# One product instead of two in the feed-forward of a batch-by-batch kernel, and the next batch's heads made earlier in the round

## The chip, the cores and the metric

The kernel runs on one core of one Trainium2 chip. The metric is the device time in microseconds of one execution. The kernel before was run three times. One further execution was profiled, and every row below comes from it.

## The reference, cut to what matters

An input x of 8 batches, 512 tokens and 256 features goes through four layers, each with a residual sum: an RNN, an LSTM, an attention block with a feed-forward, and a block of experts. The change is in the third. There a vector is mapped by `logmap0` and `expmap0`, which scale it by a function of its norm; between two such steps only a factor for each token is left.

```python
def plin(x, w, b):
    return expmap0(logmap0(x) @ w + b)
...
q = _to_heads(plin(xm, w_q, b_q))          # k and v alike
...
attn_out = plin(_from_heads(out_h), w_o, b_o)
x = mobius_add(residual, expmap0(g_msa * logmap0(attn_out)))
residual = x
xn = layer_norm(logmap0(x))
xm = expmap0(xn * (1 + sc_mlp) + sh_mlp)
ff = plin(plin(xm, w_f1, b_f1), w_f2, b_f2)   # w_f1 [256, 1024], w_f2 [1024, 256]
return mobius_add(residual, expmap0(g_mlp * logmap0(ff)))
```

There is no non-linear function between the two feed-forward matrices. With z = logmap0(xm) and u = z W1 + b1, the second `plin` needs u W2, a row of 256 for each token, and the norm of u, one number for each token. The last layer passes all tokens through a shared expert and through two of four further experts, chosen for each batch; each has a 256x1024 and a 1024x256 matrix.

## The kernel before, in words

The first part of the program (to about 1200 us) runs both recurrences and makes the attention's inputs. The second part works in nine rounds. Round b makes the attention block of batch b (called front, rounds 0 to 7) and the experts of batch b-1 (rounds 1 to 8) together. Nothing is scheduled by a planner: each engine has one function (`tensor_round`, `vector_round`, `scalar_round`, `gpsimd_round`, `sync_round`), and the order of its lines is the order of the engine's queue. Engines meet at named semaphores: `pe.wait_ge(*at("zsT_hi", b))` waits until the instruction that raises `zsT_hi` in round b is done.

A batch's 512 tokens are NQ = 4 tiles (q) of 128 partitions. The 256 features are KC = 2 blocks (k), the 1024 hidden units FC = 8 blocks (m). `steps`, `up` and `down` are the experts' products, 24 of each in a round; TensorE takes them between the front's own steps. A round goes as follows:

- Attention: scores (L1368), exponentials (L2032), values (L1383), transposes of the results, up to `o_t`, with which z is complete.
- Transposes, the product by wo (L1435), then a long chain on VectorE (`mobius_products`, `mobius_factors`, `mobius_sum`, then the norm: `moments`, `log_norm`, `normalise`, `norm_ratio`). ScalarE helps with squares, tanh and logarithm, GpSimd with powers (L2111). The result is z, scaled for each token (L1889).
- Transposes of z (L1314), copied to zT by ScalarE (first half, L2053) and VectorE (second half, L1891).
- Feed-forward: for each m two products of 512 columns, W1 against zT (L1478), ScalarE's bias (L2057) and square (L2059), VectorE's running sum of the squares (L1901), and four products of 256 columns with W2 (L1470). At the end four products with a column of ones add the squares over the partitions (L1489).
- Beside the feed-forward the next batch's heads are made: squares (L1971), sums (L1727, L1735), the power, roots (L1975), factors (L1740 to L1758), values (L2143), scaled q and k (L1764), their high parts in fp16 (L1982) and low parts (L1772).
- A second mobius chain gives the block's output (L1929, `x_out`). TensorE transposes the high and low parts (L1353, `split_transposes`), and the copies of these (`splT_moved`) are what the next round's scores wait for.

The heads' squares are written over the tiles of the attention's results (`hsq`, `oT` and `O` share `spl`), so they can't be made before z is complete. Round 0 has no experts' products; there `kept_busy` puts products that nobody reads into the longest waits. 

## Time and profile before

| | us |
|---|---|
| median of three runs | 2486.86 (2485.87 to 2488.44) |
| profiled execution, first to last instruction | 2483.3 |
| median less that span | 3.6 |
| TensorE busy in the profile | 2358.1 (95%) |
| VectorE busy | 1570.9 (63%) |
| ScalarE busy | 1350.9 (54%) |
| GpSimd busy | 569.8 (23%) |
| mean granted clock of TensorE | 0.991 |
| HBM traffic | 39 GB/s over the span |

The profiled execution's own time is known only as its span; what lies around it is not listed apart. Busy times overlap between engines. Matmuls are pipelined, so their durations overlap too, and starts are the better measure.
### The profile page before, as it was taken

To read this page: it belongs to the slowest core of one execution; us is meant where nothing else is said; L and a number is where in the kernel's file an instruction comes from. 1 tells how busy PE (TensorE), PEld (TensorE's weight loads), DVE (VectorE), ACT (ScalarE), POOL (GpSimd) and SP (SyncE) were. 2 spreads that over 40 slices of the span, in tenths; PEclk is the share of its full clock that TensorE was granted. 3 is DMA by queue.
4 is the path that set the end of the run, shared out by engine and by line. 5 is a ranking of instruction groups with operands and counts; after the bars stand their busy time and mean duration, and the time that the engine had idled before them with its cause. 6 is when DMAs were issued, how large, how long until landed. Compare 5 with 4: busy or idle time off the path is not lost.

```text
span 2483.3 us, 96145 instructions
## 1 busy us (share of the span) xinstructions
PE 2358.1 (95%) x39648; PEld 1570.9 (63%) x39648; DVE 1570.9 (63%) x7207; ACT 1350.9 (54%) x4515; POOL 569.8 (23%) x1177
## 2 busy tenths in 40 slices
PE   8899999999999999999868999999999999999999
PEld 6677777777777777776333665646556465564666
DVE  5777777777777877777466546546465464655330
ACT  4555555555555555555748556565555665556432
POOL 0222222332223222232222203222031221212100
PEclk9999999999999999999979999999999999999999
DMA  4111111110000000000103002030020301102020
GB/s 114 33 36 42 32 40 42 32 30 25 30 27 29 27 27 30 26 23 15 65 0 115 1 14 110 0 124 1 33 92 1 124 1 52 72 1 98 1 81 9
DMA packets 51880, 102.74 MB, mean 41 GB/s; under 512 B 10468, under 2 KB 33380, under 8 KB 47348
## 3 DMA queue, kind: packets, MB, share of 16 engines
q1 hardware_dynamic: 48036, 94.06, 11.2%
q8 instruction: 315, 5.16, 0.9%
q10 hardware_dynamic: 3408, 2.52, 0.3%
q14 instruction: 121, 0.99, 0.1%
HBM read 75.53 MB, written 21.04 MB: 39 GB/s over the span
## 4 chain that ended last, share of the span: by engine, by line
PE 42%; DVE 4%; ACT 3%; issue 2%; POOL 1%; DVEq 0%; ACTq 0%
PE bank L1262 13%; PE bank L1276 12%; PE bank L1470 4%; PE bank L1478 4%; ACT pexp L2032 2%; PE bank L1383 2%; PE bank L1368 1%; PE bank L1435 1%; PE bank L1297 1%; POOL hs L2111 1%; PE bank L1353 1%; PE bank L1314 1%; DVE x L1595 0%; DVE x L1598 0%; DVE spl L1786 0%
## 5 line engine op out<-in xcount | busy, mean ns | idle before, releaser
L135 PE MATMUL psFI<-wh,Hs 128*8 128x128 f32 (+3 forms) x8192 | 324.8, 276 | 60.5 <-DVE Hs L250 47.1
L135 PE MATMUL psOR<-wh,RH 128*16 128x128 f32 (+3 forms) x8320 | 321.4, 272 | 2.5 <-ACT RH L338 2.1
L135 PEld LDWEIGHTS psFI<-wh,Hs 128*8 128x8 f32 (+3 forms) x8192 | 182.2, 99 | 178.9 <-DVE Hs L250 178.4
L2032 ACT ACTIVATE pexp<-bank 128x1024 f32<-128x1024 f32 x256 | 244.2, 1022 | 33.8 <-PE bank L1368 33.6
L338 ACT ACTIVATE RH<-RT 128x16 f32<-128x16 f32 x512 | 111.0, 217 | 261.3 <-DVE RT L254 261.3
L1262 PE MATMUL bank<-x3T,ew 128*128 128x512 f32 x512 | 239.2, 594 | 0.0
L329 ACT ACTIVATE sFI<-FIT 128x32 f32<-128x32 f32 x512 | 118.6, 232 | 200.3 <-DVE FIT L234 195.5
L234 DVE STREAM_TRANSPOSE FIT<-psFI 128x128 f32<-128x128 f32 x512 | 162.3, 317 | 101.0 <-PE psFI L135 98.5
L135 PEld LDWEIGHTS psOR<-wh,RH 128*16 128x16 f32 (+1 forms) x8320 | 205.6, 104 | 5.1 <-ACT RH L338 3.7
L135 PE MATMUL psG<-wh,Hs 128*8 128x64 f32 (+3 forms) x8192 | 208.3, 219 | 0.0
L1276 PE MATMUL bank<-ew,hidden 128*128 128x256 f32 x864 | 201.0, 379 | 0.0
L1276 PEld LDWEIGHTS bank<-ew,hidden 128*128 128x128 f32 x864 | 163.5, 190 | 53.5 <-issue 35.4
L2111 POOL TENSOR_TENSOR hs<-hs,half 128x16 f32<-128x16 f32 x32 | 92.9, 2904 | 371.8 <-DVE hs L1799 371.8
L782 PE MATMUL psB<-wqkv,zrT 128*128 128x128 f32 x720 | 175.8, 326 | 0.0
L135 PEld LDWEIGHTS psG<-wh,Hs 128*8 128x8 f32 (+3 forms) x8192 | 174.7, 100 | 0.0
L135 PE MATMUL psOR<-wx,XX 128*32 128x128 f32 (+1 forms) x4160 | 168.8, 278 | 2.4 <-DMA XX<-in_xT 2.4
L335 ACT ACTIVATE tC<-cc 128x16 f32<-128x16 f32 x512 | 111.3, 217 | 104.7 <-DVE cc L243 103.7
L1951 ACT ACTIVATE hidden<-bank,eb1s 128x512 f32<-128x512 f32 x128 | 87.5, 684 | 130.9 <-PE bank L1262 129.1
L2111 POOL TENSOR_TENSOR S<-acc,half 128x4 f32<-128x4 f32 (+2 forms) x47 | 69.4, 1477 | 376.0 <-ACT dump L1964 138.1
L782 PEld LDWEIGHTS psB<-wqkv,zrT 128*128 128x128 f32 x720 | 107.0, 188 | 72.9 <-issue 70.4
L1262 PEld LDWEIGHTS bank<-x3T,ew 128*128 128x128 f32 x512 | 95.8, 190 | 73.7 <-issue 68.9
L250 DVE TENSOR_TENSOR Hs<-oT,tC 128x16 f32<-128x16 f32 x512 | 90.4, 177 | 75.7 <-ACT tC L335 1.5
(358 smaller groups left out, 4631.3 us busy)
## 6 DMA issues: line engine op xcount, KB each, us to landing
ew<-in_ew SPq DMA_DIRECT2D x32, 1024.0 KB, 9.6
qkv_scratch<-qkvr SPq DMA_DIRECT2D x31, 384.0 KB, 2.7
big<-qkv_scratch SPq DMA_DIRECT2D x7, 1536.0 KB, 7.6
XX<-in_xT SPq DMA_DIRECT2D x31, 256.0 KB, 2.7
x_scratch<-xr SPq DMA_DIRECT2D x32, 128.5 KB, 2.4
x<-x_scratch SPq DMA_DIRECT2D x8, 514.0 KB, 8.8
ada<-ada_scratch SPq DMA_DIRECT2D x8, 512.0 KB, 8.4
out_x<-x SPq DMA_DIRECT2D x7, 512.0 KB, 3.3
```

The costliest lines, as they stand in the source:

```text
L135: last = pe.matmul(bank[32 * j:32 * j + width, :], state(k), weights[:, k, j, cols], start=False, stop=k == KC - 1, tile_position=(0, 32 * ...
L234: dve.transpose(flat(R.FIT), R.psFI[g % 2]).then_inc(sem["fiT"], 1)
L329: act.activation(R.sFI[:, :, :, 1].rearrange("p g (k b) -> p (g k) b", k=KC), R.FIT[:, :, at_four:at_four + NB], ACT.Sigmoid).then_inc(sem ...
L335: act.activation(R.tC[:, :, :], by_block(second_scan(R.cc)), ACT.Tanh).then_inc(sem["tC"], 1)
L338: act.activation(r_of(i), R.RT[:, :, at_pair:at_pair + NB], ACT.Tanh).then_inc(sem["tR"], 1)
L782: last = pe.matmul(self.psB[:, half * P:(half + 1) * P], self.zT[:, k, :], self.wqkv[:, k, n * D + half * P:n * D + (half + 1) * P], start ...
L1262: last = pe.matmul(bank(4 + i % 2), M.expert(n)[0][:, k, m * P:(m + 1) * P], M.x3T[:, k, :], start=k == 0, stop=k == KC - 1)
L1276: last = pe.matmul(y_bank(q), M.hidden[:, i % HIDDEN, q * P:(q + 1) * P], M.expert(n)[1][:, m, :], start=m == 0 and (y_bank == M.last_bank ...
L1470: last = pe.matmul(bank(2 + q // 2)[:, (q % 2) * D:(q % 2 + 1) * D], M.uT[:, m, q * P:(q + 1) * P], W["wf2"][:, m, :], start=(m == 0 and q ...
L1478: last = pe.matmul(bank(m % 2), W["wf1"][:, k, m * P:(m + 1) * P], M.zT[:, k, :], start=k == 0, stop=k == KC - 1)
L2032: up(act.activation(M.pexp[:, n % 2, 2 * pr:2 * pr + 2, :], M.PS[pr][:, :, :], ACT.Exp, scale=1.0 / math.sqrt(HD)), "exps")
L2111: pool.tensor_tensor(out, base, exponent, ALU.pow).then_inc(M.sem(name), 1)
```

## The change

The feed-forward keeps one matrix of 1024 rows and 512 columns, `wf` = [W2 | W1 transposed], in place of the two. In round 0 TensorE multiplies it by W1 once: `gram` = W1 [W2 | W1 transposed], 256 x 512, kept in SBUF for all batches. The bias gives two rows, b1 W2 and 2 b1 W1-transposed, and one number, b1 b1. Each batch then takes four times two products of zT with `gram`. The left 256 columns are z W1 W2, to which a row is added. The right 256, multiplied by z and added up, are the square of the norm of z W1, to which VectorE adds the bias's part.

The heads' work is moved on VectorE, ScalarE and GpSimd: squares and sums beside the product by wo, roots and factors into the norm, the values and the scaled q and k before the copy of zT, high parts behind it, low parts between the second `mobius_factors` and `mobius_sum`. The squares' unread results now go over the exponentials' tile. Round 0's copies of the transposes are split as in the other rounds (five of eight on VectorE).

```diff
+    def gram(k):
+
+        for m in range(FC):
+            last = pe.matmul(bank(4 + k), W["wf"][:, m, D + k * P:D + (k + 1) * P], W["wf"][:, m, :], start=m == 0, stop=m == FC - 1)
+        last.then_inc(M.sem("gram_ps"), 1)
+
+    def gram_of_bias():
+
+        pe.wait_ge(*at("wide", b))
+        for m in range(FC):
+            last = pe.matmul(bank(6), M.bias_wide[:, m, :], W["wf"][:, m, :], start=m == 0, stop=m == FC - 1)
+        last.then_inc(M.sem("gram_ps"), 1)
+        for m in range(FC):
+            last = pe.matmul(bank(7)[:, 0:1], M.bias_wide[:, m, :], W["bf1"][:, m:m + 1], start=m == 0, stop=m == FC - 1)
+        last.then_inc(M.sem("gram_ps"), 1)
...
-            if a == 0 and hp2 in (0, 2):
-                pe.wait_ge(*at("a" if hp2 else "ss_f", batch - 1))
+            if a == 0:
+                pe.wait_ge(*at("ff_bias", batch - 1, hp2 + 1))
...
         output_transposes(0)
         back(H // 4 - 1)
+        if not experts:
+            gram(0)
...
         if not experts:
-            pe.wait_ge(*at("ratio2", b))
-            kept_busy(2)
+            gram(1)
+            gram_of_bias()
+            pe.wait_ge(*at("gram", b))
...
-        def second(m):
-            pe.wait_ge(*at("u", b, m + 1))
-            for q in range(NQ):
-                last = pe.matmul(bank(2 + q // 2)[:, (q % 2) * D:(q % 2 + 1) * D], M.uT[:, m, q * P:(q + 1) * P], W["wf2"][:, m, :],
-                                 start=(m == 0 and q % 2 == 0), stop=m == FC - 1, skip_group_check=True)
-            return last
-
-        for m in range(FC):
-            if m >= 2:
-                pe.wait_ge(*at("u", b, m - 1))
+        for q in range(NQ):
             for k in range(KC):
-                last = pe.matmul(bank(m % 2), W["wf1"][:, k, m * P:(m + 1) * P], M.zT[:, k, :], start=k == 0, stop=k == KC - 1)
-            last.then_inc(M.sem("u_ps"), 1)
-            if m:
-                second(m - 1)
+                last = pe.matmul(bank(q), M.zT[:, k, q * P:(q + 1) * P], M.gram[:, k, :], start=k == 0, stop=k == KC - 1)
+            last.then_inc(M.sem("ff_ps"), 1)
         if experts:
             up(FC + LEAD + 3)
-        second(FC - 1).then_inc(M.sem("ff_ps"), 1)
-        if experts:
             down(FC + 3)
-        pe.wait_ge(*at("u_ss", b))
-        for q in range(NQ):
-            last = pe.matmul(bank(0)[:, q:q + 1], M.uss[:, q * P:(q + 1) * P], M.ones[:, 0:1], start=q == 0, stop=True, skip_group_check=True)
-        last.then_inc(M.sem("utot_ps"), 1)
         if experts:
...
+        heads = b + 1 < NB
+        if heads:
+            for q in range(NQ):
+                head_sums(b + 1, q)
+            head_totals(b + 1)
...
         normalise(N, z, M.ada25[:, 1, :], b)
+        if heads:
+            head_factors(b + 1)
         norm_ratio(N, b)
         dve.wait_ge(C.sem, C.n)
         for q in range(NQ):
             up(dve.tensor_scalar(z[:, q, :], z[:, q, :], N.s1[:, q:q + 1], None, ALU.mult), "zs")
+        if not experts:
+            dve.wait_ge(*at("gram", b))
+        for q in range(NQ):
+            dve.wait_ge(*at("zs", b, q + 1))
+            if q:
+                dve.wait_ge(C.sem, C.n)
+            C.link(dve.tensor_tensor_reduce(out=M.dump_dve[:, :], in0=z[:, q, :], in1=M.ff_rows[:, D:], scale=1.0, scalar=M.bias_square[:, :],
+                                            op0=ALU.mult, op1=ALU.add, accum_out=S[:, 9, q:q + 1]))
+        if heads:
+            for q in range(NQ):
+                scaled(b + 1, q)
         dve.wait_ge(*at("zsT_ps", b, 2))
         up(dve.tensor_copy(M.zT[:, 1, :], bank(1)), "zsT_hi")
...
+        def linear_outputs(q):
+
+            dve.wait_ge(*at("ff_ps", b, q + 1))
+            dve.wait_ge(C.sem, C.n)
+            C.link(dve.tensor_tensor_reduce(out=M.dump_dve[:, :], in0=z[:, q, :], in1=bank(q)[:, D:], scale=1.0, scalar=S[:, 9, q:q + 1],
+                                            op0=ALU.mult, op1=ALU.add, accum_out=acc[:, 7, q:q + 1]))
+            up(dve.tensor_tensor(M.w[:, q, :], bank(q)[:, 0:D], M.ff_rows[:, 0:D], ALU.add), "ff_bias")
+
+        for q in range(NQ):
+            linear_outputs(q)
+        dve.wait_ge(C.sem, C.n)
+        up(dve.tensor_scalar(acc[:, 7, :], acc[:, 7, :], 0.0, None, ALU.max), "ss_f")
...
         mobius_factors(M.norm2.X2, 1)
+        if heads:
+            for q in range(NQ):
+                low_parts(b + 1, q)
         mobius_sum(1)
         for q in range(NQ):
             if q == 0:
                 dve.wait_ge(C.sem, C.n)
             up(dve.tensor_tensor(M.x1[:, q, :], M.x1[:, q, :], M.x[b % 2][:, q, :], ALU.add), "x_out")
-        if heads and experts:
+        if heads:
             for a, hp2 in SPLIT_B:
                 splT_moved(b + 1, a, hp2)
...
+        hidden(1, 2, 3)
+        if b + 1 < NB:
+            act.wait_ge(*at("o_t", b))
+            for q in range(NQ):
+                heads_squared(b + 1, q)
+        hidden(4)
+        if not experts:
+            gram_moved(0)
         mobius_squares(0, lambda: None)
         hidden(5, 6)
         tanh(0)
+        if not experts:
+            gram_moved(1)
         mobius_scaled(M.x[b % 2], 0)
         hidden(7, 8)
         logarithm(M.norm2, b)
+        if b + 1 < NB:
+            head_roots(b + 1)
+            act.activation(M.exp_scratch[:, :], M.mhalf[:, 0:1], ACT.Gelu_apprx_tanh)
+        if not experts:
+            bias_rows_moved()
...
-        for m in range(FC):
-            act.wait_ge(*at("u_ps", b, m + 1))
-            up(act.activation(M.uT[:, m, :], bank(m % 2), ACT.Identity, bias=W["bf1"][:, m:m + 1]), "u")
-            act.wait_ge(*at("u", b, m + 1))
-            up(act.activation(M.usq[:, m, :], M.uT[:, m, :], ACT.Square), "u_sq")
-            if b + 1 < NB:
-                if m < 2:
-                    heads_squared(b + 1, 2 * m)
-                    heads_squared(b + 1, 2 * m + 1)
-                if m == 2:
-                    head_roots(b + 1)
-                    act.activation(M.exp_scratch[:, :], M.mhalf[:, 0:1], ACT.Gelu_apprx_tanh)
-                if m >= 5:
-                    high_parts(b + 1, m - 5)
         if b + 1 < NB:
-            high_parts(b + 1, NQ - 1)
+            for q in range(NQ):
+                high_parts(b + 1, q)
...
+    if front and not experts:
+        pool.tensor_copy(M.bias_wide, M.W["bf1"][:, :].unsqueeze(2).to_broadcast([P, FC, P])).then_inc(M.sem("wide"), 1)
     if front:
         for g in range(H // 4):
             power(M.hs[:, 2, :, 4 * g:4 * g + 4], M.hs[:, 0, :, 4 * g:4 * g + 4], M.half[:, 0:4 * NQ].rearrange("p (q h) -> p q h", h=4), at("ss_o", b, g + 1), "root_o")
         power(S[:, 8, :], acc[:, 7, :], root, at("ss_t", b), "pow_o")
+        if b + 1 < NB:
+            head_norms(b + 1)
...
```

VectorE takes out of its queue the seven sums of squares (L1901) and the interleaving of the heads' steps with them.

TensorE's queue around the feed-forward of round 1, before. `z` and `zT` are the block's rows and their transposes, `ew_0` an expert's weights, `pexp` holds the hidden units u.

```order
L1314 MATMUL bank<-I,z 128x128
L1276 MATMUL bank<-ew_0,hidden 128x256 [waits s_hidden]
L1276 MATMUL bank<-ew_0,hidden 128x256 x3
L1478 MATMUL bank<-zT,W_wf 128x512 [waits s_zsT_hi,s_zsT_lo]
L1478 MATMUL bank<-zT,W_wf 128x512 x3
L1470 MATMUL bank<-W_wf,pexp 128x256 [waits s_u]
L1470 MATMUL bank<-W_wf,pexp 128x256 x3
L1478 MATMUL bank<-zT,W_wf 128x512 [waits s_u]
L1478 MATMUL bank<-zT,W_wf 128x512
```

The same place now:

```order
L1314 MATMUL bank<-I,z 128x128
L1276 MATMUL bank<-ew_0,hidden 128x256 [waits s_hidden]
L1276 MATMUL bank<-ew_0,hidden 128x256 x3
L1488 MATMUL bank<-gram,zT 128x512 [waits s_zsT_hi,s_zsT_lo]
L1488 MATMUL bank<-gram,zT 128x512 x7
L1262 MATMUL bank<-x3T,ew_0 128x512 [waits s_hidden]
L1262 MATMUL bank<-x3T,ew_0 128x512
```

Sixteen and thirty-two products have become eight, with the same wait ahead of them, and the experts follow at once.

VectorE's queue from the norm to the copy of zT in a round with experts, before. `S` and `hs` hold factors for each token and head, `big` is the next batch's q, k and v.

```order
L1659 SCALAR_TENSOR_TENSOR z<-z,S,ada 128x256 x4
L1663 TENSOR_SCALAR S<-S 128x4
L1516 RECIPROCAL S<-S 128x4
L1518 SCALAR_TENSOR_TENSOR S<-S 128x4
L1889 TENSOR_SCALAR z<-z,S 128x256 x4
L1891 COPY zT<-bank 128x512
```

The same stretch now, the first and last of the nine factor instructions and one of the four sums shown:

```order
L1661 SCALAR_TENSOR_TENSOR z<-z,S,ada 128x256 x4
L1742 TENSOR_SCALAR S<-S 128x4x3
...
L1760 TENSOR_TENSOR hs<-hs,S 128x192
L1665 TENSOR_SCALAR S<-S 128x4
L1518 RECIPROCAL S<-S 128x4
L1520 SCALAR_TENSOR_TENSOR S<-S 128x4
L1898 TENSOR_SCALAR z<-z,S 128x256 x4
L1905 ISA dump_dve,S<-z,ff_rows,bias_square 128x256
L1905 ISA S 128x1
...
L1766 TENSOR_TENSOR big<-big,hs 128x256 x8
L1911 COPY zT<-bank 128x512
```

The factors stand ahead of the ratio, and the sums against the bias row and all eight scalings ahead of the copy.

TensorE in round 0 from z's last transposes to the feed-forward, before and now:

```order
L1326 MATMUL bank<-I,z 128x128 x4
L1435 MATMUL bank<-W_wo,zT 128x256 x8
L1321 MATMUL bank<-W_wf 128x512 x5
L1314 MATMUL bank<-I,z 128x128 x8
```

```order
L1326 MATMUL bank<-W_wf 128x512 x8
L1342 MATMUL bank<-I,z 128x128 x4
L1453 MATMUL bank<-W_wo,zT 128x256 x8
L1326 MATMUL bank<-W_wf 128x512 x8
L1333 MATMUL bank<-W_wf,hidden 128x512 x8
L1336 MATMUL bank<-W_bf,hidden 128x1 x8
L1321 MATMUL bank<-W_wf 128x512 x3
L1314 MATMUL bank<-I,z 128x128 x8
```

The products of the matrices stand ahead of z's last transposes and behind the product by wo, in place of two of the five unread ones.

## Rows read from the trace of the kernel before

**Rows 1.** Stretches of round 2: length, each engine's busy time, granted clock, DMA share, GB/s.
```profile
1472.00:1513.00 41.00, 38.32 (x261) 13.23 (x260) 22.53 (x76) 34.18 (x39) 6.86 (x3) 1.00 0.52 187
1513.00:1626.00 113.00, 113.00 (x462) 76.61 (x461) 63.24 (x193) 57.56 (x121) 25.48 (x22) 1.00 0.00 1
```

**Rows 2.** Timeline of TensorE, round 2: start us, us, engine, line, what, count.
```profile
1559.21 3.60 PE L1478 MATMUL bank<-zT,W_wf 128*128 128x512 f32 x8
1562.64 1.89 PE L1470 MATMUL bank<-W_wf,pexp 128*128 128x256 f32 x8
1564.37 1.88 PE L1478 MATMUL bank<-zT,W_wf 128*128 128x512 f32 x4
...
1585.03 1.88 PE L1262 MATMUL bank<-x3T,ew 128*128 128x512 f32 x4
1586.74 1.89 PE L1470 MATMUL bank<-W_wf,pexp 128*128 128x256 f32 x8
1588.47 1.89 PE L1276 MATMUL bank<-ew,hidden 128*128 128x256 f32 x8
1590.20 0.95 PE L1489 MATMUL bank<-ones_,uss 128*128 128x1 f32 x8
1591.01 1.96 PE L1262 MATMUL bank<-x3T,ew 128*128 128x512 f32 x4
...
1611.75 1.95 PE L1353 MATMUL bank<-I,spl 128*128 128x128 f16 x32
```

**Rows 3.** Timeline of VectorE, round 2, with the idle time before.
```profile
1525.82 1.66 DVE L1668 SCALAR_TENSOR_TENSOR z<-bank,S,W_bo 128x256 f32<-128x256 f32 x4 [3.98 <-PE bank L1435]
...
1549.87 0.69 DVE L1663 TENSOR_SCALAR S<-S 128x4 f32<-128x4 f32 x1 [2.82 <-POOL S L2111]
...
1551.27 2.05 DVE L1889 TENSOR_SCALAR z<-z,S 128x256 f32<-128x256 f32 x4
1557.68 0.69 DVE L1891 COPY zT<-bank 128x512 f32<-128x512 f32 x1 [4.36 <-PE bank L1314]
...
1565.94 1.81 DVE L1727 TENSOR_REDUCE hs<-spl 128x48 f32<-128x768 f32 x2
...
1577.20 1.61 DVE L1764 TENSOR_TENSOR big<-big,hs 128x256 f32<-128x256 f32 x2
...
1580.85 1.28 DVE L1772 TENSOR_TENSOR spl<-big,spl 128x512 f16<-128x512 f32 x2
...
1582.65 0.75 DVE L1764 TENSOR_TENSOR big<-big,hs 128x256 f32<-128x256 f32 x2
```

**Rows 4.** Stretches of round 2 cut at VectorE's instructions, columns as in rows 1.
```profile
1528.73:1531.03 2.30, 2.30 (x11) 1.80 (x10) 1.73 (x9) 1.48 (x7) 1.31 (x1) 1.00 0.00 0
1572.95:1576.68 3.73, 3.73 (x15) 2.52 (x14) 3.45 (x11) 1.38 (x3) 0.00 (x0) 1.00 0.00 0
1591.18:1606.88 15.70, 15.70 (x53) 9.98 (x53) 12.07 (x49) 9.18 (x30) 3.91 (x4) 1.00 0.00 0
```

**Rows 5.** Timeline of ScalarE, round 2.
```profile
1542.36 0.21 ACT L2004 ACTIVATE S<-S 128x4 f32<-128x4 f32 x1 [0.78 <-DVE S L1637]
...
1562.38 1.56 ACT L1971 ACTIVATE spl<-big 128x768 f32<-128x768 f32 x2
```

**Rows 6.** Timeline of GpSimd, round 2.
```profile
1549.81 2.84 POOL L2120 TENSOR_TENSOR x<-x,weighted 128x256 f32<-128x256 f32 x4
...
1576.76 3.55 POOL L2143 TENSOR_TENSOR vt<-big,hs 128x256 f32<-128x256 f32 x4 [5.80 <-DVE hs L1758]
```

**Rows 7.** Timeline of TensorE, round 0.
```profile
1245.84 1.11 PE L1326 MATMUL bank<-I,z 128*128 128x128 f32 x4 [6.26 <-DVE z L1816]
```

**Rows 8.** Stretches of round 0, columns as in rows 1.
```profile
1248.00:1250.00 2.00, 2.00 (x5) 1.64 (x6) 0.16 (x1) 0.00 (x0) 0.00 (x0) 0.50 0.00 0
1277.50:1306.95 29.45, 28.57 (x104) 19.21 (x104) 20.51 (x37) 21.18 (x33) 6.21 (x5) 1.00 0.00 1
1306.95:1321.90 14.95, 9.60 (x70) 5.92 (x70) 12.78 (x51) 12.76 (x30) 3.02 (x2) 0.67 0.42 142
```

More of the change, by code:

```diff
@@ L420, in __init__ @@
         self.of = {}
-        for name, shape in (("wo", [P, KC, D]), ("wf1", [P, KC, FF]), ("wf2", [P, FC, D]),
+        for name, shape in (("wo", [P, KC, D]), ("wf", [P, FC, 2 * D]),
                             ("sw1", [P, KC, FF]), ("sw2", [P, FC, D]), ("gate_w", [P, 3 * KC, E]),
@@ L1320, in kept_busy @@
         for _ in range(n):
-            pe.matmul(bank(4), W["wf1"][:, 0, 0:P], W["wf1"][:, 1, 0:T], start=True, stop=True)
+            pe.matmul(bank(4), W["wf"][:, 0, 0:P], W["wf"][:, 1, :], start=True, stop=True)
+    def gram(k):
[10 more added lines that the diff above has]
+        last.then_inc(M.sem("gram_ps"), 1)
     def output_transposes(k):
@@ L1664, in norm_ratio, with mobius_products @@
         C.link(clipped_ratio(N.s1, N.n_, N.t0, C))
-    def mobius_products(banks, bias, gate, xa, nth):
+    def mobius_products(made, bias, gate, xa, nth):
         for q in range(NQ):
-            up(dve.scalar_tensor_tensor(z[:, q, :], bank(banks[q // 2])[:, (q % 2) * D:(q % 2 + 1) * D], S[:, 7, q:q + 1], bias[:, :], ALU.mult, ALU.add), "a")
+            up(dve.scalar_tensor_tensor(z[:, q, :], made(q), S[:, 7, q:q + 1], bias[:, :], ALU.mult, ALU.add), "a")
         for q in range(NQ):
@@ L1892, in vector_round @@
     if front:
-        heads = b + 1 < NB
-        if heads:
-            head_sums(b + 1, 0)
-            head_sums(b + 1, 1)
-        for m in range(1, FC):
-            dve.wait_ge(*at("u_sq", b, m + 1))
-            if m > 1:
-                dve.wait_ge(*at("u_ss", b, m - 1))
-            up(dve.tensor_tensor(M.uss, M.usq[:, 0, :] if m == 1 else M.uss, M.usq[:, m, :], ALU.add), "u_ss")
-            if heads and m == 1:
-                head_sums(b + 1, 2)
-                head_sums(b + 1, 3)
-                head_totals(b + 1)
-            if heads and m == 3:
-                head_factors(b + 1)
-            if heads and m >= 4:
-                scaled(b + 1, m - 4)
-            if heads and m >= 5:
-                low_parts(b + 1, m - 5)
-        if heads and experts:
-            low_parts(b + 1, NQ - 1)
-        dve.wait_ge(*at("utot_ps", b))
-        up(dve.tensor_copy(acc[:, 7, :], bank(0)[:, 0:NQ]), "ss_f")
-        if heads and not experts:
-            low_parts(b + 1, NQ - 1)
+        def linear_outputs(q):
[8 more added lines that the diff above has]
+        up(dve.tensor_scalar(acc[:, 7, :], acc[:, 7, :], 0.0, None, ALU.max), "ss_f")
         dve.wait_ge(*at("pow_f", b))
@@ L1929, in vector_round @@
             up(dve.tensor_tensor(M.x1[:, q, :], M.x1[:, q, :], M.x[b % 2][:, q, :], ALU.add), "x_out")
-        if heads and experts:
+        if heads:
             for a, hp2 in SPLIT_B:
@@ L2013, in splT_moved, with gram_moved, bias_rows_moved @@
         for a, hp2 in groups:
-            if batch == 1 or (a, hp2) not in SPLIT_B:
+            if (a, hp2) not in SPLIT_B:
                 act.wait_ge(*M.of_heads("splT_ps", batch, 4 * a + hp2 + 1))
                 up(act.copy(M.splT[:, a, 2 * hp2:2 * hp2 + 2, :].rearrange("p j t -> p (j t)"), bank(hp2).bitcast(fp16)), "splT_B" if (a, hp2) in SPLIT_B else "splT_A")
+    def gram_moved(k):
+        act.wait_ge(*at("gram_ps", b, k + 1))
+        up(act.copy(M.gram[:, k, :], bank(4 + k)), "gram")
+    def bias_rows_moved():
+        act.wait_ge(*at("gram_ps", b, 4))
+        up(act.copy(M.ff_rows[:, 0:D], bank(6)[:, 0:D]), "gram")
+        up(act.activation(M.ff_rows[:, D:], bank(6)[:, D:], ACT.Identity, scale=2.0), "gram")
+        up(act.copy(M.bias_square[:, :], bank(7)[:, 0:1]), "gram")
     def x3T_moved():
@@ L2087, in scalar_round @@
         hidden(19, 20)
-        if experts and b + 1 < NB:
+        if b + 1 < NB:
             splT_moved(b + 1, (0, 0), (0, 2))
         hidden(21, 22)
-        if experts and b + 1 < NB:
+        if b + 1 < NB:
             splT_moved(b + 1, (1, 0))
@@ L2148, in gpsimd_round @@
         power(S[:, 8, :], acc[:, 7, :], root, at("ss_t", b), "pow_o")
+        if b + 1 < NB:
+            head_norms(b + 1)
         mobius_power(0)
```

36 lines of the change are left out of this document (14 added, 22 removed).

## Prediction

> **What bounds the kernel now.** I read the stretches of one steady round first, then TensorE's timeline in it, then VectorE's, ScalarE's and GpSimd's, then round 0. A round lies between the first score product of one batch and that of the next. Its first 41 us (attention) are shared: TensorE is busy for 38.32 us and ScalarE for 34.18. In the next 113 us TensorE is busy for 113.00 us, VectorE for 63.24, ScalarE for 57.56, at a granted clock of 1.00 (the 2.4 GHz level) and with no transfers [rows 1]. So in the part of the round that the change touches TensorE alone sets the time, and what leaves its queue is worth its full length, as long as the others still hand over in time. Seven of the nine rounds (1 to 7) have this shape; round 0 has no experts' products to lie beside the chain, and round 8 has no feed-forward.
>
> **What leaves TensorE in a steady round.** I go by start to start, since the durations overlap. The feed-forward's first products start at 1559.21 and the experts' next one at 1585.03: 25.82 us. Its last second-stage group takes from 1586.74 to 1588.47, 1.73 us, and the sums of squares from 1590.20 to 1591.01, 0.81 us. Together 28.36 us [rows 2]. (Each fp32 matmul stands twice in the trace: x8 are four of them.) In their place come eight fp32 products 512 wide with a 128x128 stationary tile. Four such take from 1559.21 to 1562.64, 3.43 us [rows 2], so eight take 6.86. TensorE's queue gets 28.36 - 6.86 = 21.50 us shorter. As TensorE is without a gap there, that is the gain, less what it now waits.
>
> **What is late next: the second half of zT.** TensorE needs VectorE's copy of zT before the new product. Before, it arrived at 1559.21 and did not wait [rows 2]. VectorE now has more ahead of that copy. Term by term, in round 2:
> - Squares of the next heads' input: 1.56 us for two on ScalarE [rows 5], 3.1 for four, in the gap before the product by wo is done. VectorE idles there for 3.98 us [rows 3] and now reduces four times 0.905 (1.81 for two [rows 3]), and one small total. It ends about 0.3 us after 1525.82. Bounds: 0 if it fits, 1.5 if each sum waits for its square. I take 0.3.
> - Factors: the nine instructions take 3.73 us [rows 4]. They go before the ratio, where VectorE idles for 2.82 us on GpSimd's power [rows 3]. The part that doesn't fit is 0.9, and with the first 0.3 and GpSimd's additions beside it I take 1.5 for the two items together. ScalarE's root, with two table loads, goes after its logarithm at 1542.36 [rows 5]; it pushes two Gelus by some 2 us and the four squares of the norm by about 0.3, which is less than VectorE's own delay. TensorE needs these Gelus two steps later, so I cost them at nothing; uncovered, they would be 1.9.
> - Four products with a sum, against the bias row: 2.30 us for four of this kind [rows 4].
> - Eight scalings: 0.75 for two with GpSimd quiet, so 3.0; 1.61 for two beside its values' products, so 6.4 [rows 3, 6].
> - Then the copy, 0.69 [rows 3], as it was.
> The scaling of z starts at 1551.27 and takes 2.05 us with GpSimd busy [rows 3, 6]. So: 1551.27 + 1.5 + 2.05 + 2.30 + 3.0 + 0.7 + some 0.2 of handing over = 1561.0, which is 1.8 us after 1559.21. GpSimd's products for the values (3.55 us [rows 6]) now start once its additions end, near 1553, and lie on the end of the scaling of z and on the sums instead of on the eight scalings. I add 0.7 for it: TensorE waits 2.5 us in each of rounds 1 to 6. Bounds: 1.0 (no disturbance, squares fit) and 6.0 (all eight scalings at the disturbed price).
>
> On that disturbance: two scalings took 0.75 us alone and 1.61 beside GpSimd [rows 3, 6]. The Trainium skill (SBUF — State Buffer, Who interferes with whom) says that a VectorE instruction with two SBUF inputs and a GpSimd instruction that reads SBUF exclude each other for the whole instruction. The trace agrees with it in direction. By that rule alone the sums against the bias row would each be blocked too, and the wait would come out near 3.5 us and not 2.5, worth 6 us over six rounds; it is inside the range.
>
> **Is the rest in time?** The four outputs q are consumed while the next product runs: about 1.1 us of VectorE each (0.57 for the sum [rows 4], an addition at the price of a scaling, 0.38 [rows 3], and handing over) against 1.7 us of TensorE. The sum of squares is then ready at 1559.2 + 2.5 + 6.9 + 1.2 = 1569.8 instead of 1591.18, 21.4 us earlier. From it to the block's output VectorE takes 15.70 us [rows 4], and the low parts now lie inside it: eight at 0.64 (1.28 for two [rows 3]), 5.1 us. The low parts end about 1587. TensorE reaches their transposes at 1611.75 - 19.0 = 1592.7 [rows 2]: 6 us of slack, so I cost this move at nothing; if the low parts came 10 us later it would be 4 us a round. ScalarE loses sixteen instructions and gets the casts back, from 57.56 busy in 113 [rows 1]. Weights and the next batch's input arrive within the attention part, DMA share 0.52 there and 0.00 after it [rows 1], so the earlier squares find their input.
>
> So a round with next heads gains 21.50 - 2.5 = 19.0 us, six times: 114.0. Round 7 makes no heads: only the sums are added, 2.3 us on VectorE against the 4.36 us that it idled for the transposes [rows 3]. It gains 21.5.
>
> **Round 0.** Here the chain through VectorE sets the end, and nothing lies beside it.
> - Eight of the products of the matrices start where TensorE idled for 6.26 us [rows 7] and take 6.86: 0.6 late. But TensorE then enters the product by wo without having idled. Before, it was granted 0.50 (1.2 GHz) there [rows 8], after that idle time. The transposes and this product gain some 1.5. VectorE's four sums limit it, so I take 0.5 gained in all.
> - The others (eight, and eight with the bias, 13.7 us, and eight small ones) lie beside the norm, where only products that are thrown away stood. ScalarE's three small copies of them come ahead of its squares of the norm; at no more than the 0.69 us of the copy of zT each they are 2.1 us, and the factors' 1.5 us on VectorE cover most of it. Nothing, at the most 0.6.
> - From the copy of zT to the sum of squares: 29.45 us before [rows 8]. The copy comes later by 1.5 (factors) + 0.9 (scaling of z, now beside GpSimd, an estimate: half of its 2.05) + 2.3 + 3.0 = 7.7, less the 0.5: 7.2. TensorE idles for it, and part of the new product may run at 1.2 GHz: 6.86 + 2. With the last outputs, 1.2, and the copy with its handing over, 0.9, it is 7.2 + 8.9 + 1.2 + 0.9 = 18.2. Gain 11.2.
> - From the sum of squares to the next scores: 14.95 us before [rows 8]. The low parts (5.1) and VectorE's five copies of the transposes, done early before, now come into it; a copy at the 0.69 of zT's [rows 3] makes 3.4. Loss 8.5.
> Round 0: about 2.7 gained; between 8 lost (the product wholly at 1.2 GHz, the copies one behind the other) and 7 gained.
>
> **Sum.** 114.0 + 21.5 + 2.7 = 138.2 us. The profiled execution's span is 2483.3 us, giving 2345.1; the median of the runs is 3.6 above that span, which I take as fixed: 2486.9 - 138.2 = 2348.7 us.
>
> **Rivals.**
> - The clock falls in the new wait. In the steady rounds TensorE never waits as long as in my forecast, and after 6.26 us without work its clock was 0.50 [rows 7, 8]. Were it to fall at each wait for zT, the new product would take 13.7 us and not 6.9: 6 x 6.9 = 41 us lost, 2390 us. Against it: the gap is under half of that one. The Trainium skill (TensorE: Matmul & The Clock Gate, HAM oscillation — how this bites in real kernels) says that a wait in every iteration can make every next burst start cold. Whether 2.5 us do it no row here shows.
> - VectorE takes over the end of the round: the low parts or the output come after TensorE has reached their transposes. For it: all the heads' work that lay beside 28 us of products is now beside the norm and 7 us. Against it: the 6 us of slack. With 10 us more on VectorE, 4 us are lost in six rounds: 2373 us.
> - Slower than before: the clock falls at that wait and stays at 1.2 GHz. The 138 us gained are used up once 138 / 6 = 23 us of work in each of six rounds run at half speed. Behind the wait stand 1626.0 - 19.0 - (1559.2 + 2.5) = 45 us of the round [rows 1, 2]; were all of it at that level, the loss would be 6 x 45 = 270 us: about 2619. Against it: TensorE has work without a gap after the wait, and in round 0 the clock was back at 1.00 over the stretch from the copy of zT on [rows 8].
> - The shorter queue is not what the time follows, because something else had to arrive anyway: about 2480 us. The 113.00 of 113.00 speaks against it [rows 1].
>
> **Chances.** Forecast 0.81, clock at each wait 0.07, VectorE at the end 0.08, slower 0.02, nothing gained 0.02. The forecast's own range comes from its bounds: waits of 1.0 to 6.0 us (9 less, 21 more) and round 0 (4 less, 11 more): 2335 to 2380. I hold 2334 to 2378, which leaves out the first rival and a bit of the forecast. This kernel's measurement can't tell less than 0.2% (5 us) from no change. Faster 0.97, the same 0.01, slower 0.02.
>
> **What would show it.** In the changed profile: L1488's eight products in about 6.9 us, then the experts at once; an idle time of TensorE of about 2.5 us before them in rounds 1 to 6, ended by VectorE's copy of zT, and none in round 7; a clock of 1.00 there; rounds of about 135 us where they were 41 + 113 [rows 1]; no wait before the split transposes of rounds 1 to 6; round 0 about as long as before. Wrong it would be if the wait for zT is over 6 us, if TensorE shows 0.50 in a steady round, or if it idles before the transposes of the low parts or of the block's output.

## The result and the profile after

The median went from 2487.0 to 2344.5 us (after: four runs, 2343.05 to 2345.88; before: four, 2485.87 to 2488.44), a ratio of 0.9425 (95% interval 0.9414 to 0.9436). That is 142.5 us less, where 138.2 were forecast; 2348.7 was predicted. The profiled execution's span is 2341.3 us, 142.0 less than before, at a mean granted clock of 0.991. TensorE is busy for 2207.2 us of it (94%), VectorE for 1581.1 (68%).

Where it went, by start times on TensorE: up to round 0's first score product 1.4 us were lost (1202.94 before, 1204.37 after; the other profiles scatter about as much). From there to round 1's product by wo 4.55 were gained. From that to round 7's product by wo it was 117.34, which is 19.56 for each of six rounds, and in the rest 21.54.

First the stretches of round 2 of the kernel after, in the columns of [rows 1]; the round now lasts from 1450.13 to 1584.19 us.

```profile
1450.00:1491.00 41.00, 38.68 (x259) 13.15 (x258) 23.20 (x77) 33.68 (x37) 7.87 (x3) 1.00 0.52 187
1491.00:1584.00 93.00, 91.20 (x375) 60.44 (x373) 63.79 (x206) 46.40 (x105) 23.42 (x22) 1.00 0.00 1
```

The attention part is as it was. The rest is 93 us instead of 113 [rows 1], TensorE is busy in 91.20 of them, and the missing 1.8 us are one wait. Here it is in TensorE's timeline, after, round 2 (start, duration, line, what, count, idle time before and who ended it):

```profile
1499.15 3.62 PE L1453 MATMUL bank<-W_wo,zT 128*128 128x256 f32 x16
...
1534.47 1.89 PE L1276 MATMUL bank<-ew,hidden 128*128 128x256 f32 x8
1538.16 7.11 PE L1488 MATMUL bank<-gram,zT 128*128 128x512 f32 x16 [1.80 <-DVE zT L1911]
1545.10 1.88 PE L1262 MATMUL bank<-x3T,ew 128*128 128x512 f32 x4
...
1569.20 1.95 PE L1369 MATMUL bank<-I,spl 128*128 128x128 f16 x32
```

The new product takes 6.94 us from start to start in place of the 28.36 of both old ones and the sums of squares [rows 2]. The transposes of the low parts (L1369) show no wait. The wait's 1.80 us are counted from the modelled end of the products before; start to start it costs 3.69 - 1.72 = 1.97, since eight such entries otherwise take 1.72. So 28.36 - 6.94 - 1.97 = 19.45, and the rounds show 19.56.

VectorE in the same round, after; what was beside 28 us of products now stands before the copy of zT:

```profile
1498.74 3.52 DVE L1729 TENSOR_REDUCE hs<-spl 128x48 f32<-128x768 f32 x4
1502.37 0.35 DVE L1737 TENSOR_REDUCE acc<-hs 128x12 f32<-128x192 f32 x1
1502.80 1.66 DVE L1670 SCALAR_TENSOR_TENSOR z<-bank,S,W_bo 128x256 f32<-128x256 f32 x4
...
1526.92 0.81 DVE L1758 SCALAR_TENSOR_TENSOR hs<-hs 128x192 f32<-128x192 f32 x1
1527.76 0.77 DVE L1760 TENSOR_TENSOR hs<-hs,S 128x192 f32<-128x192 f32 x1
1528.45 0.69 DVE L1665 TENSOR_SCALAR S<-S 128x4 f32<-128x4 f32 x1
...
1529.85 2.56 DVE L1898 TENSOR_SCALAR z<-z,S 128x256 f32<-128x256 f32 x4
1532.33 0.47 DVE L1905 CUSTOM_DVE_ANT_0 dump_dve<-z,ff_rows,bias_square 128x256 f32<-128x256 f32 x1
...
1534.64 2.77 DVE L1766 TENSOR_TENSOR big<-big,hs 128x256 f32<-128x256 f32 x8
1537.33 0.68 DVE L1911 COPY zT<-bank 128x512 f32<-128x512 f32 x1
...
1558.30 4.90 DVE L1774 TENSOR_TENSOR spl<-big,spl 128x512 f16<-128x512 f32 x8
```

GpSimd beside it, after:

```profile
1526.79 3.00 POOL L2135 TENSOR_TENSOR x<-x,weighted 128x256 f32<-128x256 f32 x4
1529.76 2.50 POOL L2160 TENSOR_TENSOR vt<-big,hs 128x256 f32<-128x256 f32 x4
```

The four sums of the squares end just before the first addition from the banks, which starts 3.65 us after the product by wo, as before (3.66). GpSimd's work now lies on the last factors and the scaling of z. The eight scalings of q and k run alone: 2.69 us from start to start, 0.34 each, where two took 1.61 beside GpSimd and 0.75 without [rows 3].

Round 0, TensorE after:

```profile
1240.88 7.03 PE L1326 MATMUL bank<-W_wf 128*128 128x512 f32 x16
1247.75 0.60 PE L1342 MATMUL bank<-I,z 128*128 128x128 f32 x4
1249.23 3.69 PE L1453 MATMUL bank<-W_wo,zT 128*128 128x256 f32 x16 [0.88 <-DVE zT L1870]
...
1273.35 5.49 PE L1321 MATMUL bank<-W_wf 128*128 128x512 f32 x6 [5.02 <-ACT bias_square L2038]
...
1286.33 8.77 PE L1488 MATMUL bank<-gram,zT 128*128 128x512 f32 x16 [5.26 <-DVE zT L1911]
1307.91 0.37 PE L1369 MATMUL bank<-I,spl 128*128 128x128 f16 x2 [12.80 <-DVE spl L1774]
```

The first matrix products fill the 6.26 us of [rows 7], and the product by wo takes 3.69 us. Before, it took 5.09, with a granted clock of 0.50 in its first 2 us [rows 8]. Against that stand two waits: 5.02 us for ScalarE's copies of the matrices, and 5.26 for zT, after which the new product takes 8.77 instead of 7.1. The stretch of the unread products behind the first of them shows the clock at 0.55, and ScalarE's timeline shows why the copies (L2036) are late: the early root stands in front of them, with a table load before it and one behind it:

```profile
1274.00:1280.00 6.00, 5.67 (x10) 1.85 (x8) 5.62 (x15) 0.89 (x6) 3.35 (x5) 0.55 0.00 0
```

```profile
1269.53 1.28 ACT L1986 ACT_TABLE_LOAD   x1
...
1271.21 1.28 ACT L2081 ACT_TABLE_LOAD   x1
1272.50 0.20 ACT L2081 ACTIVATE exp_scratch<-mhalf 128x1 f32<-128x1 f32 x1
1272.61 0.35 ACT L2036 COPY ff_rows<-bank 128x256 f32<-128x256 f32 x1
```

### The profile page after: what moved, and what is told of

Its sections match the earlier page's. It is cut to its first block and busy times, and to the rows that moved or that the text cites. A ratio compares the mean times of both kernels' runs of the same rounds, so it can differ in the third digit from the quotient of the medians.

```text
span 2341.3 us, 94850 instructions
## 1 busy us (share of the span) xinstructions
PE 2207.2 (94%) x39004; PEld 1452.3 (62%) x39004; DVE 1581.1 (68%) x7316; ACT 1257.8 (54%) x4381; POOL 560.5 (24%) x1178
## 5 line engine op out<-in xcount | busy, mean ns | idle before, releaser
L2054 ACT ACTIVATE pexp<-bank 128x1024 f32<-128x1024 f32 x256 | 244.3, 1023 | 36.1 <-PE bank L1384 35.9
L240 DVE TENSOR_TENSOR gw<-sFI,cc 128x16 f32<-128x16 f32 x512 | 90.4, 176 | 72.4 <-ACT sFI L329 3.0
```

The source lines that it names most:

```text
L240: dve.tensor_tensor(second_scan(R.gw), second_scan(R.sFI[:, 0]), second_scan(R.cc), ALU.mult).then_inc(sem["w"], 1)
L2054: up(act.activation(M.pexp[:, n % 2, 2 * pr:2 * pr + 2, :], M.PS[pr][:, :, :], ACT.Exp, scale=1.0 / math.sqrt(HD)), "exps")
```

## The experiments

All ten were run beside the kernel before (medians of 2486.2 to 2486.6 us in three sets of runs); ratios are to it. "After" is the changed kernel at 2344.5. "A round" is the distance between the products by wo of two rounds, 134.1 us in the kernel after.

### Does TensorE's queue set the rounds? (e1_product_twice)

```diff
         for q in range(NQ):
-            for k in range(KC):
-                last = pe.matmul(bank(q), M.zT[:, k, ...], M.gram[:, k, :], ...)
+            for _ in range(2):
+                for k in range(KC):
+                    last = pe.matmul(bank(q), M.zT[:, k, ...], M.gram[:, k, :], ...)
```

> The changed kernel, with each of the four pairs of products by gram taken twice (the second time to the same result). Theory, TensorE's queue sets the steady rounds: eight more products are 7.1 us in each of rounds 1 to 7 and some 7 to 9 in round 0, so 2344.5 + 57 = 2401 us, and rounds of 141.2 us where the changed kernel has 134.1. Rival, VectorE's chain behind the product is nearly as long as TensorE's queue: it is pushed by the same 7.1 us, so the time is the same, but TensorE then idles before the split transposes or the output's transposes. Rival, part of TensorE's time is hidden: less than 40 us in all, 2344 to 2384.

Measured: 2397.4 us (2396.26 to 2400.38), ratio 0.9644 (0.9628 to 0.966), 52.9 over after. TensorE, round 2:

```profile
1550.71 13.97 PE L1489 MATMUL bank<-gram,zT 128*128 128x512 f32 x32 [1.80 <-DVE zT L1912]
```

Five of the six rounds are 140.9 us, 6.8 longer. The sixth is 142.7; its doubled product ran slow (see the last section). The wait is the same, and none appears before the split transposes. By the profile the second part is 57.0 us longer, which is what was expected; the time shows 52.9, in part because what comes before the rounds was 1.8 us shorter in this execution. What is added to TensorE's queue is paid in full; so was what left it. The theory that something else had to arrive anyway is out.

### What the wait for zT costs (e2_scaled_after_copy, e3_both_after_copy)

e2 moves the eight scalings behind the copy of zT, e3 also the four sums against the bias row:

```diff
-        if heads:
-            for q in range(NQ):
-                scaled(b + 1, q)
         dve.wait_ge(*at("zsT_ps", b, 2))
         up(dve.tensor_copy(M.zT[:, 1, :], bank(1)), "zsT_hi")
+        if heads:
+            for q in range(NQ):
+                scaled(b + 1, q)
```

> The changed kernel, with VectorE's eight scalings of the next q and k behind its copy of zT instead of ahead of it. Theory, the 1.8 us that TensorE waits in rounds 1 to 6 and most of the 5.3 us of round 0 are these scalings standing ahead of the copy: the wait goes in rounds 1 to 6 (10.9 us), and in round 0 it falls by 2.5 to 3 and with it some of the product's slow clock: 2344.5 - 14 = 2330 us. Rival, the scalings then lie in front of VectorE's work on the outputs and cost there what they save here: 2340 to 2346. The four outputs take VectorE 4.4 us beside 7.1 us of products, so there is room for 2.7 us; I expect the first.

> As the run before, and the four sums against the bias row behind the copy too. Theory: in rounds 1 to 6 there is no wait left to take, so they stay; in round 0 the copy comes another 2.4 us earlier, and the product starts without its clock having fallen: 2330 - 2.4 - 1 = 2327 us. Rival, 5 us of VectorE behind the copy are more than the product hides, and the second chain starts later: then round 0 gains nothing over the run before (2330), while the steady rounds stay, having some 6 us of slack.

e2: 2328.6 us (2326.8 to 2329.1), 0.9365 (0.9349 to 0.9381), 15.9 less than after. Rounds 1 to 6 have no wait, and most are 132.0 to 132.1 us. TensorE, round 2 of e2:

```profile
1530.99 7.03 PE L1488 MATMUL bank<-gram,zT 128*128 128x512 f32 x16
```

A round is 2.05 us shorter: the wait's 1.97 and 0.08 of the product, which is 7.03 without a wait and 7.11 with one. Six times that is 12.3; round 0's wait fell from 5.26 to 2.57. e3: 2325.1 us (2322.93 to 2327.34), 0.9349 (0.9334 to 0.9365). Its times can't be told from e2's; in round 0 the wait is 0.88, but the product still takes 8.80. I had counted on it being faster there.

### Does the heads' early move pay, and how much slack was there? (e4, e8, e5, e6)

e4 keeps the new product but makes the heads late: sums behind the copy of zT, factors and scalings after the second norm's ratio, and on ScalarE squares, root and high parts in front of a Gelu, `hidden(14)`. e8 puts the high parts behind Gelus 14 to 16. The core of e4 against after, and of e8 against e4:

```diff
-        if heads:
-            head_factors(b + 1)
         norm_ratio(N, b)
...
+        if heads:
+            head_factors(b + 1)
+            for q in range(NQ):
+                scaled(b + 1, q)
         dve.wait_ge(*at("ff_bias", b))
...
         hidden(13)
         if b + 1 < NB:
             for q in range(NQ):
+                heads_squared(b + 1, q)
+            head_roots(b + 1)
+            act.activation(M.exp_scratch[:, :], M.mhalf[:, 0:1], ACT.Gelu_apprx_tanh)
+            for q in range(NQ):
                 high_parts(b + 1, q)
         hidden(14)
```

```diff
-            for q in range(NQ):
-                high_parts(b + 1, q)
         hidden(14)
         mobius_squares(1, lambda: hidden(15))
         hidden(16)
+        if b + 1 < NB:
+            for q in range(NQ):
+                high_parts(b + 1, q)
         tanh(1)
```

> The changed kernel's single product, but the next heads made behind the copy of zT, as before the change (squares and sums beside the product, factors and scalings ahead of the second chain). Theory, the single product gives the gain and the heads' move only a little: no wait for zT (1.8 us gained), but the low parts end about 4 us after TensorE reaches their transposes: 2 us lost a round, and some 2 in round 0: 2344.5 + 14 = 2358 us. Rival, the heads' work needs the product's old length as cover, so that without the move half of the gain is lost: 10 us a round, 2344.5 + 65 = 2410 us.

> As the run with the heads made late, but ScalarE's high parts behind the experts' Gelus 14 to 16 and not ahead of them. In that run TensorE waited 5.7 us a round for a Gelu (34.8 us), which stood behind the high parts, which waited for VectorE's scalings. Theory, that place in ScalarE's queue was the loss: without it only the 2 us a round that I had expected are left, from the low parts: 2355 to 2365 us. Rival, VectorE's heads' work behind the copy is what is too long: the wait turns up ahead of the split transposes instead, 5 us a round, and the time stays at 2377.

e4: 2377.3 us (2375.54 to 2377.86), 0.9563 (0.9547 to 0.9579). e8: 2363.5 (2362.72 to 2364.8), 0.9503 (0.9486 to 0.952). TensorE's waits in e8 (who waited for what: us in total, times, longest), then e4's round 2 on TensorE and on ScalarE:

```profile
PE bank L1369 <- DVE spl L1774: 24.2, 4, 21.8
PE bank L1262 <- ACT hidden L1961: 19.7, 7, 3.2
```

```profile
1559.38 3.73 PE L1262 MATMUL bank<-x3T,ew 128*128 128x512 f32 x4 [5.74 <-ACT hidden L1961]
```

```profile
1553.53 5.22 ACT L1992 CAST spl<-big 128x512 f16<-128x512 f32 x8 [8.06 <-DVE big L1766]
1558.65 0.68 ACT L1961 ACTIVATE hidden<-bank,eb1s 128x512 f32<-128x512 f32 x1
```

And ScalarE in round 2 of e8, the first square of the second chain:

```profile
1557.18 0.42 ACT L1974 ACTIVATE pexp<-z 128x256 f32<-128x256 f32 x1 [8.78 <-DVE z L1670]
```

I had looked for the loss at the transposes of the low parts. (In e8 they are late in round 0 only: 24.2 us of waits there, 15.2 in the kernel after.) In rounds 1 to 6 it is elsewhere: the Gelu stands behind the high parts, these behind VectorE's scalings, and TensorE's next products wait for the Gelu, 5.74 us in each round of e4, which is 139.9 us long. In e8 what is left is again a Gelu, 3.2 us in each round, and the two products after it (x4 in the trace) take 3.15 to 3.78 us instead of 1.88. This Gelu stands behind four squares of the second chain, for which ScalarE waits 8.78 us until VectorE has made z, and VectorE has the heads' factors and scalings in front of that. So e8 came out at the time expected of it, but not by the mechanism: its rival was right that VectorE's work behind the copy is too long, and only the place where TensorE feels it was another. Made late in this way, the heads cost 19 us against after; the early move is that share of the gain. A better late placement wasn't tried.

e5 and e6 keep the kernel after and make the low parts two and three times, to the same place:

```diff
             for q in range(NQ):
+                for _ in range(1):           # 2 in e6
+                    for a in (0, 1):
...
+                        C.link(dve.tensor_tensor(lo, M.qkv[:, q, a]..., hi, ALU.subtract))
+                    dve.wait_ge(C.sem, C.n)
                 low_parts(b + 1, q)
```

> The changed kernel, with the eight low parts of the next heads made twice (the same result), 5.1 to 5.4 us more on VectorE between the second factors and sum in rounds 0 to 6. Theory, there are some 6 us of slack ahead of their transposes in a steady round: rounds 1 to 6 keep their 134.1 us, and only round 0, whose end this chain sets, is longer by 5: 2344.5 + 5 = 2350 us. Rival, no slack, VectorE's chain already ends the rounds: seven times 5, 2381 us.

> The low parts three times, 10.5 us more on VectorE. Theory: 10.5 less 6 of slack, so TensorE waits some 4.5 us ahead of the split transposes in rounds 1 to 6, and 10.5 in round 0: 2344.5 + 27 + 10.5 = 2382 us. If the slack is really larger, nothing but round 0 shows: 2355. Rival, no slack: 2344.5 + 73 = 2418 us.

e5: 2351.4 us (2349.48 to 2353.5), 0.9452 (0.9435 to 0.9469). e6: 2398.2 (2397.34 to 2398.97), 0.9642 (0.9625 to 0.9659). Round 2 on TensorE, e5 and then e6 with the granted clock of the last entry's stretch:

```profile
1576.41 1.62 PE L1369 MATMUL bank<-I,spl 128*128 128x128 f16 x26 [0.25 <-DVE spl L1774]
```

```profile
1588.24 0.28 PE L1369 MATMUL bank<-I,spl 128*128 128x128 f16 x2 [1.69 <-DVE spl L1774]
1592.11 2.96 PE L1369 MATMUL bank<-I,spl 128*128 128x128 f16 x26 [3.58 <-DVE spl L1774]
```

```profile
1592.11:1595.00 2.89, 2.89 (x27) 2.89 (x28) 2.85 (x8) 1.77 (x2) 0.00 (x0) 0.50 0.00 0
```

The slack can be read from the kernel after itself. There the low parts end at 1558.30 + 4.90 = 1563.20, and TensorE reaches their transposes at 1569.20: 6.0 us, as forecast. One more set of eight makes the low parts end 7.3 us later (71.35 us after the product by wo instead of 64.04), and not 4.9, mostly because GpSimd's additions, from 1569.52 on, now lie on them. VectorE, e5, round 2: two added ones beside GpSimd, and the last two (two take 1.29 us alone):

```profile
1569.81 2.35 DVE L1941 TENSOR_TENSOR spl<-big,spl 128x512 f16<-128x512 f32 x2
...
1575.66 1.29 DVE L1774 TENSOR_TENSOR spl<-big,spl 128x512 f16<-128x512 f32 x2
```

The first transposes don't need the last low parts, so of the 7.3 us only 0.25 are a wait. Five of e5's six rounds are 134.5 to 134.8 us; the sixth is 136.3, with a slow product (last section). In e6 the low parts end 12.5 us later, and the waits are 5.3 us, but the rounds 141.1 to 142.4, on average 7.7 longer than after. The remaining 2.4 us are the clock: after the 3.58 us wait 26 transposes take 2.96 us instead of 1.62, at 0.50, and products behind them are slow too. I had not expected that; six times 2.4 us are 14 of the 16 us by which e6 missed.

### Does the clock fall in a longer wait? (e7_sums_three_times)

```diff
-        for q in range(NQ):
+        for q in [q for q in range(NQ) for _ in range(3)]:
             dve.wait_ge(*at("zs", b, q + 1))
-            if q:
+            if True:
                 dve.wait_ge(C.sem, C.n)
```

> The changed kernel, with each of the four sums against the bias row made three times ahead of the copy of zT: some 4.8 us more of wait for TensorE, 6.6 instead of 1.8 in rounds 1 to 6 and 10 in round 0. Theory: TensorE pays the wait one for one, eight times, and 38 to 40 us; in round 7, which had none of the wait but some room, 3 to 5. If the clock also falls to 1.2 GHz in this wait, as it does in round 0 (the product took 8.8 us there and 7.1 in the steady rounds), each product is longer by 1.7 to 6.9 us, 10 to 45 us more: 2394 to 2430. If it doesn't fall: 2383. After 6.3 us without work it had fallen in round 0, so I expect it to fall.

Measured: 2395.9 us (2394.36 to 2398.15), 0.9637 (0.962 to 0.9654); the mean granted clock is 0.980. TensorE in round 2 and in round 7, and the stretch of the first entry:

```profile
1553.80 8.71 PE L1488 MATMUL bank<-gram,zT 128*128 128x512 f32 x16 [6.90 <-DVE zT L1911]
...
2256.10 8.80 PE L1488 MATMUL bank<-gram,zT 128*128 128x512 f32 x16 [2.10 <-DVE zT L1911]
```

```profile
1553.80:1562.50 8.70, 8.70 (x17) 3.92 (x18) 2.48 (x9) 1.20 (x3) 0.00 (x0) 0.81 0.00 0
```

With 5.1 us more to wait, rounds are 140.8 to 142.2 us, 7.3 longer on average: 5.1 for the wait and 2.2 for products partly at 1.2 GHz (8.7 to 10.1 us instead of 7.1). So the rival of the prediction, a clock that falls in this wait, is a mechanism of this kernel; in the kernel after, at 1.8 us, it didn't act; at 6.9 it does every time. The Trainium skill (TensorE: Matmul & The Clock Gate, HAM oscillation — how this bites in real kernels) says that a gap in each iteration can make every next burst start cold. The rows agree for e7 and e6, with only part of the burst cold, and not for the kernel after, whose product in round 2 is this stretch:

```profile
1538.16:1545.10 6.94, 6.94 (x17) 3.11 (x17) 2.48 (x9) 1.71 (x4) 0.00 (x0) 1.00 0.00 0
```

### Round 0 (e9_gram_wait_later, e10_copies_first)

e9 is e3 with TensorE's wait for ScalarE's copies of the matrices moved to where they are read, and more unread products in the waits. e10 also makes round 0's five copies of the transposes ahead of the second sum.

```diff
             gram_of_bias()
-            pe.wait_ge(*at("gram", b))
+            pe.wait_ge(*at("gram", b, 1))
+            kept_busy(3)
             pe.wait_ge(*at("z2", b, 1))
             kept_busy(2)
             pe.wait_ge(*at("squares2", b))
-            kept_busy(1)
+            kept_busy(4)
...
+        if not experts:
+            pe.wait_ge(*at("gram", b))
         pe.wait_ge(*at("zsT_lo", b))
```

```diff
                 low_parts(b + 1, q)
+            if not experts:
+                for a, hp2 in SPLIT_B:
+                    splT_moved(b + 1, a, hp2)
         mobius_sum(1)
...
-        if heads:
+        if heads and experts:
             for a, hp2 in SPLIT_B:
                 splT_moved(b + 1, a, hp2)
```

> The kernel with scalings and sums behind the copy of zT, and in round 0 TensorE's wait for the copies of gram moved from ahead of the unread products to ahead of the feed-forward, with three and three unread products more in its idle times. In round 0 TensorE idled for 5.0 us for these copies, its clock was at 1.2 GHz at the unread products, and the feed-forward's product took 8.8 us where it takes 7.0 at 2.4 GHz. Theory, it is that idle time that lets the clock fall: now the product takes 7.0, 1.8 us less in all: 2325.1 - 1.8 = 2323 us, steady rounds as they are (132.0). Rival: the clock falls in the 2.4 us of small gaps at the transposes of z, then nothing changes, 2325; or the unread products come late and hold the transposes up, 2326 to 2328.

> As the run before, and in round 0 VectorE's five copies of the split transposes ahead of the second sum and the output (3.0 us) instead of behind them. Theory, round 0 ends with these copies, for which round 1's scores wait, while the output is needed only some units later: 3 us less: 2320 us. Rival, the output's transposes, 3.4 us later now, hold up the first values' products of round 1, and most of it is given back: 2322 to 2323.

e9: 2323.6 us (2322.45 to 2325.39), 0.9344 (0.9331 to 0.9357). e10: 2323.8 (2322.81 to 2326.47), 0.9348 (0.9336 to 0.9361). Stretches of round 0, first e3's unread products and its new product, then e9's norm and new product:

```profile
1273.87:1280.00 6.13, 5.80 (x8) 2.05 (x8) 5.75 (x16) 1.54 (x8) 2.83 (x4) 0.57 0.00 0
1282.47:1291.20 8.73, 8.73 (x16) 3.52 (x16) 6.72 (x25) 4.26 (x8) 0.00 (x0) 0.80 0.00 0
```

```profile
1268.00:1281.00 13.00, 9.55 (x26) 3.67 (x24) 10.65 (x32) 6.11 (x17) 4.53 (x6) 1.00 0.00 0
1281.23:1288.20 6.97, 6.97 (x16) 2.93 (x16) 6.53 (x25) 4.26 (x8) 0.00 (x0) 1.00 0.00 0
```

And the new product on TensorE, in e3 and in e9:

```profile
1282.47 8.80 PE L1488 MATMUL bank<-gram,zT 128*128 128x512 f32 x16 [0.88 <-DVE zT L1900]
```

```profile
1281.23 7.11 PE L1491 MATMUL bank<-gram,zT 128*128 128x512 f32 x16 [0.87 <-DVE zT L1903]
```

The stretch where e3 had idled 5 us and then ran at 0.57 is at 1.00 in e9, and the product takes 7.11 us behind the same wait. So in e3 it had been slow because of what TensorE did before, and not because of its own short wait. (e9 takes the idle time away and adds unread products at once; the two aren't told apart.) In the times the 1.7 us are inside the spread. In e10 round 1's scores start earlier (TensorE, e10):

```profile
1311.06 0.61 PE L1384 MATMUL bank<-splT 64*128 64x512 f16 x4
1312.48 1.45 PE L1314 MATMUL bank<-I,x 128*128 128x128 f32 x8 [0.81 <-DVE x L1946]
```

They started at 1312.37 in e9, but the output's transposes now wait for VectorE, and of 1.3 us gained 0.7 are left at the next product by wo. The times show none of it.

The best version is e9 (e3 is as good within the measurement): about 21 us, or 0.9%, faster than the changed kernel, and 6.6% faster than the one before.

## Why the prediction was right, point by point

- **TensorE's queue is 21.50 us shorter.** 28.36 - 6.94 = 21.42. The eight products take 6.94 instead of 6.86 start to start behind a wait. That TensorE's queue was the bound is shown by e1.
- **The wait for zT, 2.5 us.** It is 1.97, and this term is the one that was mis-sized most. From the first addition to the new product I had 35.9 us, and it is 35.36. The squares are in time. The factors, two of them at 0.8 us beside GpSimd where round 0 has 0.36, bring the scaling of z to 27.05 us after the addition (26.95 forecast). It takes 2.48 up to the next start instead of 2.05, the sums 2.31 (2.30), the eight scalings 2.69 instead of 3.0, and of the 0.7 that I had added for GpSimd on top nothing came but that longer scaling. The prediction's other figure, near 3.5 us with the sums against the bias row blocked too, didn't come. The Trainium skill (SBUF — State Buffer, Who interferes with whom) says that a VectorE instruction with two SBUF inputs and a GpSimd instruction that reads SBUF exclude each other. The sums begin at 1532.33, when GpSimd's last product is over (1532.26), so no row here tests it on them; the last factor, which has two such inputs, agrees in direction (0.77 us beside GpSimd, 0.36 in round 0).
- **A round gains 19.0.** 19.56, six times: 117.3 instead of 114.0. This is most of the difference of 4 us.
- **Round 7 gains 21.5.** 21.54; no wait there.
- **6 us of slack before the low parts' transposes.** 6.0 in the profile, and e5 and e6 agree with it. Costed at nothing, rightly.
- **Round 0 gains 2.7.** The terms held: the first addition came 0.97 us earlier in the round (0.5 forecast), the copy of zT 6.57 later (7.2), from the copy to the sum of squares it is 10.38 us (11.0), and from there to the next scores 23.63 instead of 14.95, a loss of 8.7 (8.5). That is 3.8 gained, and another 0.7 in round 1's attention. The copies of the matrices on ScalarE didn't delay the norm, as costed. But they let TensorE idle for 5.02 us, of which I had said nothing. e3 and e9 show that this idle time is enough for a slow product even where the wait for zT is 0.88 us; whether the 5.26 us of the kernel after would do it alone isn't tested. The slow product itself was in the forecast (6.86 + 2, measured 8.77), put down to the wait for zT only.
- **Rivals.** VectorE at the end of the round: its 10 us would have decided, 6 were free and none was needed. Clock at each wait: not at 1.8 us; its price of 6.9 us a round was too high even where it acts (1.6 to 3.0 in e7). Clock that stays low: in e7 the stretch after the wait is at 0.81 on average and the rounds lose 2.2 us, not 45. Nothing gained: out by e1.
- **Luck.** The forecast put a wait of 2.5 us and no loss in clock together. The rows at hand speak against that pair: of three products behind waits of 1.89 or 1.90 us two ran slow, and so did the one behind 2.10 us in a steady round, each by 1.7 us. Had the forecast's own wait come about, and with it this loss in each of six rounds, it would have been about 10 us more, near 2359 (an estimate from these rows, and inside the range). By these rows the clock stayed because the wait came out at 1.8 us, and the prediction had no way of knowing how near that was.

## What to carry to other kernels

Where one engine's row says 113.00 busy of 113.00, price an edit by the start-to-start times of what leaves its queue, and then walk the other engine's chain up to the handover, with every instruction that is moved before it. Then look at the one instruction that TensorE waits for, and put everything that doesn't feed it behind it: here eight scalings and four sums behind one copy gave another 19 us, of which the scalings alone gave 16. A wait of 1.8 us cost itself; waits of 3.6 and 6.9 us cost some 2 us more in clock.
